# L0's attention: the product of C with the scanned state in three fp32r passes instead of one fp32 product

## What is computed

```python
a = jnp.tanh(jnp.einsum('ble,hde->blhd', emb, Wa_w) + Wa_b)
bg = jnp.einsum('ble,hde->blhd', emb, Wb_w) + Wb_b
def step(h, ab):
    at, bt = ab
    h = at * h + bt
    return (h, h)
_, hs = jax.lax.scan(step, h0, (aT, bT))
Dx = emb @ D_w.T + D_b
out = (jnp.einsum('blhd,hkd->blhk', hs, C_w) + C_b) * Dx[:, :, None, :]
out = _ln(out, hn_g, hn_b)
sum_heads = (Dx + jnp.einsum('h,blhd->bld', head_w, out)) / nH
z = sum_heads @ Wout_w.T + Wout_b
u = z + _ln(z, norm_g, norm_b)
ffn = jax.nn.gelu(u @ ffn1_w.T + ffn1_b, approximate=False)
h_out = u + (ffn @ ffn2_w.T + ffn2_b)
return h_out @ proj_w.T + proj_b
```

## Time and profile before

| | us |
|---|---|
| median of three runs | 1163.65 |
| the three runs | 1159.08, 1163.65, 1170.48 |
| the profiled execution | 1157.41 |
| its span | 1155.7 |
| PE busy | 1012.9 (88%) |
| DVE busy | 818.6 (71%) |
| POOL busy | 643.6 (56%) |
| ACT busy | 639.3 (55%) |

### The profile page before, as it was taken

How to read it: one execution, slowest core, us unless ns; L and a number is a source line. 1 busy time by engine, 2 the same in 40 slices (tenths; PEclk the granted TensorE clock), 3 DMA queues, 4 the chain that set the end, 5 groups by cost and what they waited for, 6 DMA issues and landing times.

```text
span 1155.7 us, 16233 instructions
## 1 busy us (share of the span) xinstructions
PE 1012.9 (88%) x4744; PEld 708.9 (61%) x4744; DVE 818.6 (71%) x2327; ACT 639.3 (55%) x1265; POOL 643.6 (56%) x751
## 2 busy tenths in 40 slices
PE   6788999998979999999978989899976668989996
PEld 5335777765647667667746447777834445656663
DVE  7775886758878787888674775676744678777661
ACT  2335667765565676666543336676744345455543
POOL 4006556447998888877661026555256767663440
PEclk9899999999999999999997899999987889999998
DMA  8577767740000000000002025687710000000000
GB/s 264 193 254 250 226 213 237 255 125 24 17 12 13 14 15 12 15 5 2 1 1 67 7 71 196 214 258 225 218 50 23 24 19 28 14 24 10 10 15 23
DMA packets 63495, 105.26 MB, mean 91 GB/s; under 512 B 7888, under 2 KB 42192, under 8 KB 63376
## 3 DMA queue, kind: packets, MB, share of 16 engines
q1 hardware_dynamic: 54320, 85.60, 22.8%
q0 software_dynamic: 9088, 18.63, 5.6%
HBM read 79.29 MB, written 26.87 MB: 92 GB/s over the span
## 4 chain that ended last, share of the span: by engine, by line
PE 48%; POOL 19%; DVE 13%; issue 11%; ACT 6%; DMA 1%; another core or an unknown queue 1%; POOLq 0%; SPq 0%; ACTq 0%; DVEq 0%
PE bank L208 6%; POOL wr L678 3%; PE bank L457 3%; PE bank L455 3%; PE bank L474 3%; POOL head_rstd L1379 3%; PE bank L456 3%; PE bank L453 3%; PE bank L472 3%; PE bank L473 3%; PE bank L1193 2%; PE bank L1153 2%; PE bank L1159 2%; POOL got L678 2%; PE bank L1199 2%
## 5 line engine op out<-in xcount | busy, mean ns | idle before, releaser
L622 POOL DMA_INDIRECT spare_all<-xs,list_row x156 | 158.0, 1013 | 237.0 <-DVE list_row L786 109.8
L858 DVE TENSOR_TENSOR hid_lo<-hid,hid_hi 128x512 fp32r<-128x512 f32 (+1 forms) x184 | 112.1, 611 | 74.1 <-ACT hid L559 44.7
L558 ACT ACTIVATE hid_hi<-bank,b_up_of 128x512 fp32r<-128x512 f32 (+1 forms) x138 | 86.7, 628 | 56.0 <-PE bank L457 36.8
L559 ACT ACTIVATE hid<-bank,b_up_of 128x512 f32<-128x512 f32 (+1 forms) x184 | 113.0, 624 | 5.0 <-issue 1.7
L678 POOL DMA_INDIRECT got<-ys,y_slots x80 | 85.9, 1074 | 44.6 <-DMA ys<-spare_all 26.0
L1272 ACT ACTIVATE gate_b<-bank,head_rstd 128x128 f32<-128x128 f32 x256 | 73.1, 370 | 63.5 <-POOL head_rstd L1379 63.0
L208 PEld LDWEIGHTS bank<-ident,spare_all 128*128 128x128 f32 x476 | 61.2, 151 | 69.6 <-issue 59.2
L208 PE MATMUL bank<-ident,spare_all 128*128 128x128 f32 x476 | 78.8, 290 | 22.1 <-DVE spare_all L401 15.7
L559 ACT ACTIVATE hid<-bank,cols_sb 128x512 f32<-128x512 f32 x64 | 44.0, 687 | 91.5 <-PE bank L453 79.1
L455 PE MATMUL bank<-xh,wr 128*128 128x512 f32 (+1 forms) x184 | 78.9, 429 | 13.2 <-issue 7.0
L1379 POOL TENSOR_TENSOR head_rstd<-head_var,neg_half 128x4 f32<-128x4 f32 x64 | 75.9, 1186 | 5.3
(11 more groups left out here) (325 smaller groups left out, 2694.2 us busy)
## 6 DMA issues: line engine op xcount, KB each, us to landing
wr<-wq SPq DMA_DIRECT2D x92, 512.0 KB
wq<-wr SPq DMA_DIRECT2D x16, 512.0 KB, 5.7
ys<-spare_all SPq DMA_DIRECT2D x32, 256.0 KB
got<-in_w_mlp SPq DMA_DIRECT2D x8, 512.0 KB, 5.6
xs<-spare_all SPq DMA_DIRECT2D x16, 256.0 KB, 2.3
spare_all<-xs,list_row POOLq DMA_INDIRECT x156
out_x<-X SPq DMA_DIRECT2D x8, 256.0 KB, 2.3
ys<-in_x SPq DMA_DIRECT2D x1, 1920.0 KB
```

The costliest lines, as they stand in the source:

```text
L559: nc.scalar.activation(hid[:, n % HC, 0:w], bank[up_bank(n)][:, 0:w], ACT.Gelu_apprx_tanh, bias=bias).then_inc(s["gelu_done"], 1)
L622: g.indirect_dma_start(out=xin[:, j % XIN, b], out_offset=None, in_=xs, in_offset=bass.IndirectOffsetOnAxis(ap=list_row[:, n:n + 1], axis=0))\
L858: v.tensor_tensor(hid_lo[:, q, 0:w], hid[:, n % HC, 0:w], hid_hi[:, q, 0:w].bitcast(F32), ALU.subtract).then_inc(s["lo_done"], 1)
```

## The change

The C weights and the scanned state are each split into a high part (fp32r) and a low part (the rest, in fp32r), and C's one fp32 product becomes three fp32r passes: high by high, low weights by high state, high weights by low state. The parts lie in `wr`, whose 12 units of 128 x 512 are free then. ScalarE makes the high parts by copying, VectorE the low ones by subtracting. Once, the weights: ScalarE behind `keep_x(0)`, VectorE in slot 0 behind the scan. For every head: `keep_hs` on ScalarE behind `share_head`, `rest_of_hs` on VectorE behind `head_stats`. TensorE waits for the low part before the first of the three passes. VectorE's scan of head q also waits for the copy of head q - 2.

```diff
+        unit = wr[:].rearrange("p r h l n -> p (r h l) n")
+        cw_parts = [unit[:, k:k + 2].rearrange("p a (g n) -> p (a g) n", n=P) for k in (4, 6)]
+        hs_hi, hs_lo = unit[:, 8:10], unit[:, 10:12]
...
             def c_of_head(q):
-                pe.wait_ge(s["hs_ready"], q + 1)
+                if q == 0:
+                    pe.wait_ge(s["w_lo_ready"], 4)
+                pe.wait_ge(s["hs_lo_ready"], q + 1)
                 if q > 0:
                     pe.wait_ge(s["o_ready"], q)
-                nc.tensor.matmul(bank[2][:], cw[:, q % NH], hs[:, q % 2], start=True, stop=True).then_inc(s["c_in"], 1)
+                w = [part[:, q % NH] for part in cw_parts]
+                nc.tensor.matmul(bank[2][:], w[0], hs_hi[:, q % 2], start=True, stop=False)
+                nc.tensor.matmul(bank[2][:], w[1], hs_hi[:, q % 2], start=False, stop=False)
+                nc.tensor.matmul(bank[2][:], w[0], hs_lo[:, q % 2], start=False, stop=True).then_inc(s["c_in"], 1)
...
+            def keep_hs(q):
+                act.wait_ge(s["hs_ready"], q + 1)
+                if q >= 2:
+                    act.wait_ge(s["c_in"], q - 1)
+                nc.scalar.copy(hs_hi[:, q % 2], hs[:, q % 2]).then_inc(s["hs_hi_ready"], 1)
+
             keep_x(0)
+            nc.scalar.copy(cw_parts[0], cw[:]).then_inc(s["w_hi_ready"], 1)
             keep_dx(0)
...
                     share_head(n - 3)
+                if n < HEADS:
+                    keep_hs(n)
                 if phase == 3 and n // NH + 1 < TILES:
...
                 if i % 2 == 1 and h == 0:
                     steps.wait()
+                if q >= 2:
+                    dve.wait_ge(s["hs_hi_ready"], q - 1)
...
+            def rest_of_hs(q):
+                dve.wait_ge(s["hs_hi_ready"], q + 1)
+                if q >= 2:
+                    dve.wait_ge(s["c_in"], q - 1)
+                v.tensor_tensor(hs_lo[:, q % 2], hs[:, q % 2], hs_hi[:, q % 2].bitcast(F32), ALU.subtract).then_inc(s["hs_lo_ready"], 1)
...
                     head_stats(n - 2)
+                if n == 0:
+                    dve.wait_ge(s["w_hi_ready"], 4)
+                    v.tensor_tensor(cw_parts[1], cw[:], cw_parts[0].bitcast(F32), ALU.subtract).then_inc(s["w_lo_ready"], 1)
+                if n < HEADS:
+                    rest_of_hs(n)
                 if phase == add_at + 1 and n // NH + 1 < TILES:
```

More of the change, by code:

```diff
@@ L1092, in mix_sems @@
                 "head_rstd", "share_ready", "added", "base_in", "base_out", "z_stats", "z_rstd", "un_ready", "u_ready", "u_in", "uT_ready",
-                "f1_in", "f1_out", "f2_in", "hT_ready", "y_in", "tile_done")}
+                "f1_in", "f1_out", "f2_in", "hT_ready", "y_in", "tile_done",
+                "hs_hi_ready", "hs_lo_ready")}
         HEADS = NH * TILES
```

## The result

The changed kernel takes 1194.76 us (median of 4 runs, 1191.85 to 1197.75) against 1164.66 for the kernel before beside it: a ratio of 1.0281, 95% interval 1.0242 to 1.0320, or 30.1 us more. I had forecast +14.2. The profiled execution took 1197.75 (span 1196.0).

A forecast was written before the change was run, and what follows sets the result against it. TensorE was taken as the bound, with a GpSimd backlog once per tile. Steady tiles +6.2, tile without fetches +2.4, last six +3.6 and opening +2.0 gave +14.2 us on 1163.65: 1178, range 1163 to 1194.

The forecast's parts named there:

- The prices: Undisturbed durations per instruction: subtraction 0.62 us, copy 0.59, fp32r pass 0.23; once, weights' cast 1.03 and subtraction 1.2.
- The bare product: C's product after the subtraction, no longer under VectorE's statistics: 1.05 us, making a head without other VectorE work 4.83.
- TensorE's 0.17 a head: Three fp32r passes cost 0.69 us against 0.86 for the fp32 pair: 0.17 saved per head wherever TensorE is the bound.
- The intervals of a tile: Eight C-to-C intervals, heads 33 to 41, each the larger of TensorE's and VectorE's time: together 43.2 us instead of 41.6.
- the tile without fetches: C products 49 to 57, without GpSimd backlog: 39.42 us becomes 41.85, +2.4.
- the last six: C products 57 to 63: 27.24 us becomes 30.9, +3.6.
- The interval with u: Fifth interval of a steady tile, where VectorE makes u after GpSimd's unchanged chain; C of head 38 at 27.6 us.
- a rival at 0.18: VectorE's subtraction and GpSimd block one another: 0.8 us in a quarter of the heads, +13 us, 1191 us; chance 0.18.
- The opening: C products 0 to 17, 86.24 us before, with slack: +2.0 us, between 0 and 5.
- up to 0.6 us shows: ScalarE's copy is hidden under VectorE's statistics; if ScalarE's head share is late, up to 0.6 us shows.
- The rival by which TensorE stays the bound: The bare product is absorbed everywhere and only the 0.17 saving counts: 1152.7 us; chance 0.15.
- The narrower range: The forecast's own range, 1168 to 1188 us, from +6.9 (no backlog, opening at nothing) and +27 (small prices at upper end).

The follow-up runs named there:

- the subtraction from PSUM: Changed kernel, but the subtraction's first input is the previous head's product in PSUM instead of the state in SBUF, except in the first head: ratio 1.0146 to before.
- the passes to fill: Changed kernel, with TensorE running three more fp32r passes in heads 1 to 16 before its wait for the subtraction, results overwritten: ratio 1.0266 to before.
- the passes alone: Against the changed kernel: scan writes fp32r, three passes read it, no copy or subtraction per head, state's low part left out: ratio 0.9940 to before.
- the small sum: Changed kernel with GpSimd's addition of the head's share cut to one column, leaving out the sum over heads: ratio 1.0115 to before.
- load alone: Changed kernel's copies and subtractions made but unused; C stays one fp32 product waiting for the scan alone: 1189.63 us, ratio 1.0179 to before.
- first passes early: Changed kernel, but TensorE's first two passes wait only for the high part, the third for the low part: ratio 1.0213 to before.
- scan ahead of o: Changed kernel, but VectorE does the carry and next scan before multiplying the last product (o): ratio 1.0230 to before.

## Why the prediction was wrong

The direction was right and the forecast's size was not: +14.2 for +30.1, and 1194.76 is just past the range's upper end of 1194. By its own steps:

- **The prices** were right. Subtraction 0.62 from start to start: 0.60, with 0.66 in the record. Copy 0.59: 0.62. fp32r passes 0.23 apart. Weights' cast 1.03 and subtraction 1.2: 1.06 and 1.20. The bare product 1.05, loop 4.83: the smallest distance of two scans is 4.83.
- **TensorE's 0.17 a head** was right where it is the bound: 6.42 to 6.25, 5.28 and 5.30 to 5.12 and 5.14.
- **The intervals of a tile** were right where nothing blocks: the tile without fetches at 42.38 for 41.85, the last six at 31.69 for 30.9, and with the subtraction from PSUM the steady tile at 42.50.
- **The interval with u** was put too long, 6.5 for 5.57: VectorE's longer loop gives GpSimd time, and its backlog had nearly melted by then (u waits 0.40 for the normalization of z). This hid part of the blocking.
- **The step that failed** is the one that gave the subtraction its undisturbed duration everywhere and left the blocking to a rival at 0.18, with 0.8 us in a quarter of the heads, +13 and 1191 us. That rival is what came: 12 of 64 heads, 15.1 us in sum, 1.26 each. Fewer and longer than I had them, nearly the same sum. It is worth 10.9 us of the stage by the one experiment that takes away nothing else. Against the kernel with the passes to fill, which ran on the same chip and has the same twelve, it is 13.0 of the stage and 12.8 of the medians (1161.54 and 1148.75), some of which those passes cost. The ratios, 1.0281 less 1.0146, give 15.7, on two chips and with a margin of some 7. I had its place as well: the subtraction "starts soon after the head's share is ready, which is also what starts that addition". That is no chance of a quarter. It is a fixed meeting, twice in each of five tiles, and the two queues written down side by side (GpSimd's gather, addition and variances from the trace before, VectorE's new order) might have shown it before any run.
- **The opening** was mis-sized: +2.0 (0 to 5) for +7.8. With the subtraction from PSUM it is +4.9, so about 3 of it is blocking: heads 4, 11 and 12 alone have 0.80 + 1.63 + 1.65. The rest lies in heads 0 to 8, 42.5 us without blocking where I had 40.0; in the interval of head 4, 7.04 us long there, the scan takes 1.70 for 1.27, ScalarE waits 3.09 for GpSimd's root with the head's share, and VectorE 1.60 for the copy behind it. The prediction had that case ("up to 0.6 us shows") and counted it at nothing; it was 1.60 there. The lower clock isn't seen to be the cause: with it at 0.96 for 0.85 heads 0 to 8 took 44.80 for 44.95.
- **The rival by which TensorE stays the bound** fell at once, and the reason given held: VectorE's loop of 3.78 and more decides. Even the passes alone gave 4.8 us, not 10.9.
- **The narrower range**, 1168 to 1188, doesn't follow from its own two sums, +6.9 and +27, which give 1170.6 and 1190.7 on the median; the measured time lies above it either way.

Trainium skill, "SBUF — State Buffer", section "Who interferes with whom": a VectorE instruction with two SBUF inputs and a GpSimd instruction that reads SBUF exclude each other. The runs agree: held 12 times of 64 with two inputs in SBUF, never of 63 with one in PSUM, at the same place. The additions stretched by a scan, 46 of 64, fit it as well: each starts inside the scan. One thing is not as the rule has it, that the later of two waits for the whole of the earlier: the subtraction at 481.57 started by the record 0.46 us before the addition at 482.03, and still ended after it. That is no single case. Seven of the twelve (heads 11, 12, 20, 27, 28, 36 and 44) started 0.17 to 0.47 before the addition and inside the gather in front of it, and they are the longest, 2.00 to 2.33, with 11.2 of the 15.1 us. The record of GpSimd's starts may be rough there, or the gather may matter; this stays open. Without the large addition, in the changed kernel with the small sum, seven subtractions started inside a gather and none was held.

Open too: what the bare product would be worth if nothing were held. The pairs that hide it (load alone, first passes early, scan ahead of o) all have other instructions held in turn, and no kernel had both the subtraction from PSUM and the early passes.

## What to carry to other kernels

Before adding a VectorE instruction with two SBUF inputs to a loop, write down what GpSimd runs at that point of the schedule. A meeting that the order fixes comes back in round after round and is no matter of chance; here it cost up to 1.67 us beside an addition of 1.27. With one input in PSUM it was gone, though in a kernel made for measuring, whose result leaves out the low part; no complete kernel here tries it. Behind the opening, a budget by engine from undisturbed durations was right to 3% in the stretches without such a meeting, so price the meetings on top of it, one by one.

## What the runs showed of the hardware

- A VectorE subtraction of 128x512 with two SBUF inputs takes 0.66 us, and in the changed kernel 0.95 to 2.33 when it meets GpSimd's 128x512 addition (1.27); it ends 0.56 after the addition. With one input from PSUM, 0.66 at the same place.
- It works both ways: GpSimd's operation of 128x4 took 565 ns in the mean beside the subtraction with two SBUF inputs, and 269 beside the one from PSUM. GpSimd's 128x512 addition took 1.65 for 1.27 when it started inside a VectorE scan, and over 1.4 in 46 of 64 heads of the changed kernel.
- A scan of 128x512 beside that addition took 1.78 for 1.28.
- Three fp32r passes from copies of the state gave TensorE 0.69 for 0.86, but with nothing else added the stage became only 4.8 us shorter, where TensorE's busy time in it fell by 9.0 (302.1 to 293.1).
- TensorE's granted clock in heads 0 to 8 was 1.00 before, 0.85 after with its waits, 0.96 with passes to fill them, and the time of that stretch was nearly the same for the last two, 44.95 and 44.80.
